# Attention on one core: one 128x1024 VectorE instruction for the low halves of the transposed probabilities in place of two of 128x512

## What is computed

```
q, k, v = (ln(x) @ W + b), 16 heads of 64
scores  = einsum('bhqd,bhkd->bhqk', q, k) / 16
mask    = triu(full((S, S), -999.0), k=S - 1)      # hits one score: query 0, key 1023
p       = softmax(scores + mask)
att     = einsum('bhqk,bhkd->bhqd', p, v)
```

## Time and profile before

| | us |
|---|---|
| median of 3 runs | 2617.53 |
| lowest, highest | 2610.24, 2617.77 |
| the profiled execution | 2612.62 |
| its span, first to last instruction | 2610.5 |

### The profile page before, as it was taken

How to read it: one execution, slowest core, us unless ns; L and a number is a source line. 1 busy time by engine, 2 the same in 40 slices (tenths; PEclk the granted TensorE clock), 3 DMA queues, 4 the chain that set the end, 5 groups by cost and what they waited for, 6 DMA issues and landing times. The chain is left out here.

```text
span 2610.5 us, 46625 instructions
## 1 busy us (share of the span) xinstructions
PE 2451.6 (94%) x14544; PEld 2105.9 (81%) x14544; DVE 1914.1 (73%) x3637; ACT 1674.2 (64%) x2887; POOL 1501.0 (57%) x1519
## 2 busy tenths in 40 slices
PE   6999969999999999999999999999999689959998
PEld 5888858888888888888888888888888488858887
DVE  5777547878778788787887887878878577646565
ACT  3444447877777777777787777777778533323333
POOL 2332157677777777777767777677776343412111
PEclk8999889999999999999999999999999899979999
DMA  4222342212222132221321222213221344220111
GB/s 159 81 96 88 138 130 73 90 41 82 79 73 89 51 94 65 69 85 61 92 89 41 80 81 72 89 41 97 65 73 49 132 148 133 77 89 31 48 48 40
DMA packets 133706, 212.85 MB, mean 82 GB/s; under 512 B 12564, under 2 KB 95816, under 8 KB 125000
## 3 DMA queue, kind: packets, MB, share of 16 engines
q1 hardware_dynamic: 133576, 211.48, 25.2%
HBM read 112.88 MB, written 48.25 MB: 62 GB/s over the span
## 5 line engine op out<-in xcount | busy, mean ns | idle before, releaser
L1165 DVE TENSOR_REDUCE a_nmax<-a_sc 128x1 f32<-128x1024 f32 x512 | 626.8, 1224 | 271.3 <-PE a_sc L1235 263.5
L1096 POOL TENSOR_SCALAR a_pr<-a_pr,a_rden 128x1024 f32<-128x1024 f32 x512 | 575.6, 1125 | 260.7 <-DVE a_rden L1170 199.2
L1026 ACT ACTIVATE a_pT<-a_tr 128x512 fp32r<-128x512 f32 x1024 | 558.9, 596 | 238.9 <-PE a_tr L1247 234.4
L1176 DVE TENSOR_TENSOR a_pT<-a_tr,a_pT 128x512 fp32r<-128x512 f32 x1024 | 650.7, 677 | 14.1 <-ACT a_pT L1026 14.1
L1268 PE MATMUL a_ov<-a_pT,a_v_s 128*128 128x512 f32 x2048 | 604.6, 417 | 1.4 <-DVE a_half L1156 1.4
L1032 ACT ACTIVATE a_pr<-a_sc,a_nmax 128x1024 f32<-128x1024 f32 x512 | 573.4, 1120 | 18.8 <-DVE a_nmax L1165 15.8
L1235 PE MATMUL a_sc<-a_k_s,a_q_s 128*128 128x512 f32 x2048 | 560.0, 395 | 2.3 <-ACT a_pr L1032 2.0
L1247 PEld LDWEIGHTS a_tr<-a_ident,a_pr 128*128 128x128 f32 x4096 | 475.5, 140 | 89.2 <-DVE a_pT L1176 14.0
L1247 PE MATMUL a_tr<-a_ident,a_pr 128*128 128x128 f32 x4096 | 535.8, 273 | 7.1 <-DVE a_pT L1176 6.1
L1235 PEld LDWEIGHTS a_sc<-a_k_s,a_q_s 128*128 128x128 f32 x2048 | 380.3, 188 | 88.6 <-ACT a_pr L1032 2.4
L1268 PEld LDWEIGHTS a_ov<-a_pT,a_v_s 128*128 128x128 f32 x2048 | 346.5, 189 | 54.1 <-issue 3.5
(11 more groups left out here) (220 smaller groups left out, 3224.4 us busy)
## 6 DMA issues: line engine op xcount, KB each, us to landing
a_z_s<-zT SPq DMA_DIRECT2D x32, 1024.0 KB, 6.6
a_k_s<-a_k_s SPq DMA_DIRECT2D x64, 512.0 KB, 5.6
a_wqk_s<-w_split SPq DMA_DIRECT2D x64, 256.0 KB, 3.0
a_v_s<-a_v_b SPq DMA_DIRECT2D x16, 1024.0 KB, 4.6
att<-a_ao SPq DMA_DIRECT2D x32, 512.0 KB, 2.9
m_att_in<-att SPq DMA_DIRECT2D x16, 1024.0 KB, 5.4
a_wv_s<-w_split SPq DMA_DIRECT2D x17, 512.0 KB, 3.7
zT<-f_zT SPq DMA_DIRECT2D x8, 1024.0 KB, 3.9
```

What stands on the lines that cost most here:

```text
L1026: act.activation(pT[:, (u // 4) % 2, 0, 4 * part:4 * part + 4, (u % 4) * P:(u % 4 + 1) * P], tr[:, part].rearrange("p (t q) -> p t q", t=4 ...
L1096: pool.tensor_scalar(pr[:, k % NP], pr[:, k % NP], rden[:, k % NP:k % NP + 1], 1.0, ALU.mult, ALU.mult).then_inc(s["normed"], 1)
L1165: dve.tensor_reduce(nmax[:, k % NP:k % NP + 1], sc[:, k % 2], AX.X, ALU.max, negate=True).then_inc(s["negmax"], 1)
L1176: dve.tensor_tensor(to[:, 1], tr[:, part].rearrange("p (t q) -> p t q", t=4), to[:, 0].bitcast(F32), ALU.subtract).then_inc(s["tr_lo"], 1)
```

## The change

VectorE's loop over the two parts goes. It waits once, for both high halves of the tile, and forms both low halves in one instruction over both banks of `tr`, that is 128x1024. At its end it adds 2 to `tr_lo`. The waits of TensorE are as they were.

```diff
                     if transposes_at(k, first, last):
                         t = (k - LAG) % ITER
-                        for part in range(2):
-                            dve.wait_ge(s["tr_hi"], 2 * (u - LAG) + part + 1)
-                            to = pT[:, (t // 4) % 2, :, 4 * part:4 * part + 4, (t % 4) * P:(t % 4 + 1) * P]
-                            dve.tensor_tensor(to[:, 1], tr[:, part].rearrange("p (t q) -> p t q", t=4),
-                                              to[:, 0].bitcast(F32), ALU.subtract).then_inc(s["tr_lo"], 1)
+                        dve.wait_ge(s["tr_hi"], 2 * (u - LAG) + 2)
+                        to = pT[:, (t // 4) % 2, :, :, (t % 4) * P:(t % 4 + 1) * P]
+                        dve.tensor_tensor(to[:, 1], tr[:].rearrange("p b (t q) -> p (b t) q", t=4),
+                                          to[:, 0].bitcast(F32), ALU.subtract).then_inc(s["tr_lo"], 2)
```

## The result

| | before | changed |
|---|---|---|
| median | 2614.11 us (4 runs) | 2746.65 us (4 runs) |
| lowest, highest | 2610.24, 2617.77 | 2745.37, 2747.94 |
| span of the profiled execution | 2610.5 | 2745.9 |

The ratio is 1.0504, with a 95% interval from 1.0491 to 1.0518: 5.0% slower. The prediction had 2728, and 2674 to 2778 as its range. One of the four runs of the changed kernel with projections in halves, further down, was in a slower state (2824.55 us, at a mean granted clock of 0.836 where all others have 0.97 to 0.98) and is left out.

What follows compares the result with a forecast made beforehand. TensorE in attention was taken as the bound. Longer transpose distances add 123 us, less 10 for z: +113 on the profiled 2612.6 gives 2726, plus 2 towards the median, 2728 us; range 2674 to 2778.

Steps and rivals of the forecast that it cites:

- (a): VectorE's low halves: one 128x1024 instruction takes 1.225 us for the pair's 1.27, saving 23 us off the path.
- (b): VectorE waits for both high halves, starting at 710.09 instead of 709.74 in the plain step; alone this delays nobody else.
- (c): Both transpose banks released together at the end: a closed loop of 3.10 us against TensorE's 2.75 in a plain step.
- Plain steps: Attention steps without a projection: 246 distances between transposes grow by 0.35 us each, 86 us.
- Steps behind a copy: 52 distances after VectorE first copies the other head's half: 3.20 us, taken as +0.37 each, 19 us.
- Loop starts: 15 distances following the start of a loop body: from 3.31 to 4.40 us, +1.1 each, 16 us.
- z: TensorE's weight-load wait for z from the DMA, used in step 17, goes: 10 of 12.4 us counted back.
- VectorE as the late engine: Rival in attention: less VectorE work removes TensorE's waits, 20 us fewer, about 2597 at best; chance 0.06 including unknown hiding.
- the lost lead: Rival at TensorE's transposes: late starts also pay 0.24 us weight-load lead, adding 46 us, 2774; chance 0.08.
- the faster instruction: Rival at VectorE's low halves: 1.12 us gives 2694, with a shorter hand-over too 2674; chance 0.10.
- the two pieces: Rival at VectorE's low halves: the edit is issued in two pieces with one release, +15 us, 2743; chance 0.04.
- the falling clock: Rival on TensorE: pauses drop plain steps to the 1.2 GHz level, 790 us more, 3400; chance 0.02.

Runs made afterwards that it cites:

- projections in halves: Changed kernel with the first half of each projection's matmuls moved to the end of the step before, except step 17's: 2671.75 us (3 runs), 1.0209 of before.

## Why the prediction was right

It was right in its sign, its place and its mechanism, and 19 us too low.

- What bounds the kernel: TensorE in attention, at a clock of 1.00, and it still is, with waits added.
- (a) VectorE's work: 1.225 us for the instruction, measured 1.221, 26 us less in all for the 23 expected. The saving was put off the path, and nothing of it is seen; the instruction itself is a term of the loop.
- (b) The wait: said to delay nobody by itself. In the changed kernel no loss by it shows beside the loop's. Alone, in steps of 2.75 us, it is false: 38 us, of which some 30 through the copy in VectorE's queue and the value matmuls that wait for it. The step looked at the next maximum in a plain step, and should have looked at a copy step and at who waits for the copy. That this didn't spoil the sum is luck: the longer steps of the loop hide it.
- (c) The loop: 3.10 expected, 3.16 measured. The mis-sized term is the hand-over from ScalarE to VectorE, 0.03 in rows 6 and 0.10 with the large instruction (737.09 to 737.19; so in 401 of the 512 tiles). It was measured on a small instruction. The other terms held: the high halves 1.09, and TensorE starts 0.06 after the low halves end and ScalarE 0.69 after that, 0.75 together for the 0.76 counted. Behind a projection, where the transposes didn't wait, ScalarE starts 0.64 after them, and the distance is 3.11.
- Plain steps: 246 by +0.35 were expected, 86 us. The 16 other steps of the table hold 241 of these and the 2 us behind the loop starts, some 87 in all, and grew by 96.9. The 153 that come first behind a projection grew by 0.37 each and 79 further ones by 0.41, which makes 7 to 8 of the 10 us; the rest is behind the loop starts and in the last iteration.
- Steps behind a copy: 19 expected, 18.3 measured for 48 of the 52. Their mean is 3.20, as forecast, but not for the reason given: into steps 8 and 16 it is 3.16 and 3.17, where VectorE is free about when it may start anyway, and into step 4 it is 3.25, because ScalarE starts its high halves 0.79 after the transposes there in place of 0.64.
- Loop starts: 16 expected, 16.6 measured. Their median is 4.33 (3.24 before) and the longest 4.59, for 4.40 forecast.
- z: 10 us back expected, 9.4 measured.
- Steps with a projection: 0 expected. They grew by about 0.04 each (4.12 to 4.16), 6 us: behind transposes that had to wait, the value matmuls start 0.85 after them (738.47, 739.32) in place of 0.79 (622.30, 623.09). With the last iteration's plain steps that class is +9.3.
- The rest, 3 us, lies outside the stretch between the transposes and wasn't looked into.

Of the rivals of the prediction, VectorE as the late engine, the lost lead, the faster instruction, the two pieces and the falling clock are all excluded by the rows above: no gain, 0.06 from low half to transposes, 1.221 us, one row a tile, 1.00. Of its signs one came out otherwise: TensorE's busy time didn't stay near 1676 but is 1721, by the way rows are counted that the result tells. The rule of the Trainium skill that speaks against the change ("Perfetto Trace Analysis", section "Matmuls": rotate the groups through the banks) was the one that decided: the wait and the release, which together take the two banks out of turn, make the whole loss with the two small instructions too (2746.5 us). Its rule on fixed costs ("VectorE: DVE Perf Modes", section "The TRN2 errata") has the sign of VectorE's busy time right, 26 us less; on the path the large instruction and the pair both came to 1.32 us from the end of the high halves.

## What to carry to other kernels

When two instructions on a buffer in two parts are made one, count the release before the overhead: write the loop from the fill of the buffer to its next fill with all parts in a row, and compare it with the other work of the bounding engine in each step, not with its mean. Here that mean was no less than the loop (20 steps of 2.75 and 12 of 4.13 give 3.27 against 3.16), and still 132 us were lost in the short steps. Making the steps alike first gets a part back, here some 74 us; the merged kernel stayed 2.1% slower than the one before. And when an engine is made to wait, look at everything queued behind it and at who waits for that: one copy in every fourth step cost some 30 us here.

## What was not expected of the hardware

- A waiting VectorE instruction of 128x1024 started 0.10 us after the high halves ended (median of 401), one of 128x512 0.03 after (median of 384 without the large instruction). With their lengths, 1.22 and 1.29 for the pair, both are done 1.32 us after them: the saving that VectorE's busy time shows (650.7 to 625.0 us) isn't there when the instruction is waited for. Why the larger one starts later stays open.
- ScalarE's copy of 128x1024 from PSUM took 1.03 us, its two of 128x512 1.09 together.
- Eight transposes that had to wait took 0.85 us up to the value matmuls (median of 328 in the changed kernel), those that didn't 0.79.
